# A decoder block on one core: the self attention runs in cycles of two pairs of heads, grouped by kind of work

## What is computed

```python
q = _split_heads(x @ Wq + bq, h)
k = _split_heads(x @ Wk + bk, h)
v = _split_heads(x @ Wv + bv, h)
scale = 1.0 / jnp.sqrt(jnp.float32(ATTN_DIM))
pattern = jnp.einsum('bhid,bhjd->bhij', k, q) * scale
prob = jax.nn.softmax(pattern, axis=-2)
out = jnp.einsum('bhis,bhid->bhsd', prob, v)
b, _, s, dv = out.shape
concat = out.transpose(0, 2, 1, 3).reshape(b, s, h * dv)
return concat @ Wo + bo
...
x = x + _L0_attn_ref(_layernorm(x, axis=-1), ...)
x = x + _L0_xattn_ref(_layernorm(x, axis=-1), ctx_1024, ctx_1024, mask_1x1xSxS2_ik1, ...)
x = x + _L0_ffn_ref(_layernorm(x, axis=-1), ...)
```

## Time and profile before

| | us |
|---|---|
| median of 3 runs | 214.42 |
| lowest and highest | 214.04, 215.87 |
| the profiled execution | 215.71 |
| its span, first to last instruction | 213.9 |
| TensorE busy in it | 198.1 (93%) |
| VectorE busy | 161.6 (76%) |
| ScalarE busy | 127.9 (60%) |
| GpSimd busy | 93.1 (44%) |

### The profile page before, as it was taken

The page is one execution under the profiler, slowest core; times in us unless marked ns, Lnnn a source line. Parts: engine busy times, 40 slices in busy tenths (PEclk is TensorE's granted clock), DMA queues, the critical chain, the costliest instruction groups (busy, mean ns, idle before and its releaser), DMA issues.

```text
span 213.9 us, 4341 instructions
## 1 busy us (share of the span) xinstructions
PE 198.1 (93%) x1544; PEld 149.2 (70%) x1544; DVE 161.6 (76%) x424; ACT 127.9 (60%) x300; POOL 93.1 (44%) x138
## 2 busy tenths in 40 slices
PE   7799997999999898997969999999898999999993
PEld 6388775676776575655637566566576899999993
DVE  2477558968685996788997999998994676458752
ACT  2385348757575556547947999999696532362320
POOL 7699935664646646205999600000120004611422
PEclk9999999999999999999996999999999999999999
DMA  6950478969945215006004100000000000000000
GB/s 204 359 162 0 150 98 93 96 70 112 122 60 166 78 40 112 0 0 222 3 14 101 34 0 3 0 5 2 0 3 0 3 0 2 3 0 28 0 0 25
DMA packets 10732, 12.67 MB, mean 59 GB/s; under 512 B 864, under 2 KB 8544, under 8 KB 10640
## 3 DMA queue, kind: packets, MB, share of 16 engines
q1 hardware_dynamic: 9896, 11.15, 26.0%
q10 hardware_dynamic: 720, 1.06, 1.5%
q0 software_dynamic: 96, 0.20, 0.4%
HBM read 10.96 MB, written 1.44 MB: 58 GB/s over the span
## 4 chain that ended last, share of the span: by engine, by line
PE 77%; DVE 12%; issue 4%; DMA 2%; POOL 1%; ACT 1%; SPq 0%; POOLq 0%; DVEq 0%
PE ps L844 12%; PE ps L806 10%; PE ps L735 7%; PE ps L865 7%; PE ps L722 7%; PE ps L750 6%; PE ps L784 6%; PE ps L766 6%; PE ps L639 5%; PE ps L652 4%; DVE q_t L1062 3%; DMA wk<-in_L_xattn_Wk 2%; PE ps L621 2%; DVE prob_t L1135 1%; DVE low L1052 1%
## 5 line engine op out<-in xcount | busy, mean ns | idle before, releaser
L444 POOL TENSOR_TENSOR prob<-prob,rec 128x512 f32<-128x512 f32 x32 | 32.6, 1039 | 24.2 <-DVE rec L1117 24.2
L1062 DVE CUSTOM_DVE_ANT_0 q_t<-ps,mask_add 128x512 f32<-128x512 f32 x64 | 41.3, 681 | 1.7 <-PE ps L766 1.7
L544 ACT ACTIVATE prob<-ps,low 128x256 f32<-128x256 f32 x64 | 29.5, 474 | 18.4 <-DVE low L1052 18.4
L569 ACT ACTIVATE q_t<-q_t,low 128x512 f32<-128x512 f32 x44 | 29.4, 719 | 9.8 <-DVE low L1062 9.8
L381 POOL TENSOR_SCALAR var_eps<-mean_var 128x2 f32<-128x2 f32 (+1 forms) x5 | 1.1, 224 | 64.3 <-DVE mean_var L921 64.3
L806 PE MATMUL ps<-ident,q_t 128*128 128x128 f32 x176 | 23.3, 274 | 3.8 <-DVE place_o L1135 1.9
L806 PEld LDWEIGHTS ps<-ident,q_t 128*128 128x128 f32 x176 | 20.0, 141 | 8.7 <-issue 4.5
L1052 DVE TENSOR_REDUCE low<-ps 128x2 f32<-128x512 f32 x32 | 20.5, 683 | 6.3 <-PE ps L722 6.3
L554 ACT ACTIVATE q_t<-ps 128x512 f32<-128x512 f32 x18 | 10.6, 598 | 21.0 <-PE ps L844 21.0
L1132 DVE COPY prob_t<-ps 128x512 f32<-128x512 f32 x32 | 20.5, 680 | 1.5 <-PE ps L750 1.5
L766 PE MATMUL ps<-k_stack,q_stack 72*128 72x512 bf16 x64 | 19.6, 391 | 1.3 <-issue 1.3
(11 more groups left out here) (165 smaller groups left out, 424.8 us busy)
## 6 DMA issues: line engine op xcount, KB each, us to landing
k_stack<-k_dram SPq DMA_DIRECT2D x9, 256.0 KB
q_stack<-q_dram SPq DMA_DIRECT2D x6, 192.0 KB
wg<-in_L_ffn_w_gate SPq DMA_DIRECT2D x1, 1024.0 KB, 28.8
wu<-in_L_ffn_w_up SPq DMA_DIRECT2D x1, 1024.0 KB, 35.7
k_dram<-prob SPq DMA_DIRECT2D x1, 768.0 KB, 5.2
...
```

What stands on the lines that cost most here:

```text
L444: nc.gpsimd.tensor_tensor(pr, pr, rec1[:, s % 2, r, :].unsqueeze(2).to_broadcast([P, C, S]), ALU.mult).then_inc(s_norm1, 1)
L544: e = nc.scalar.activation(prob1[:, s % 3, r, c * S:(c + 1) * S], ps[:, 2 * (s % 2) + r, c * S:(c + 1) * S], ACT.Exp, bias=low1[:, s % 2, ...
L569: nc.scalar.activation(prob2[n % 3][:, c, :], score2[n % 2][:, c, :], ACT.Exp, bias=low2[:, n % 2, c:c + 1], scale=-1.0).then_inc(s_exp2, 1)
L1062: nc.vector.tensor_tensor_reduce(out=score2[n % 2][:, c, :], in0=ps[:, 2 * (n % 2) + c, :], in1=mask_add[:, c, :], scale=1.0, scalar=3e38, ...
```

## The change

Self attention now advances in cycles of two pairs, on every even g up to 16. In a cycle TensorE does the scores of pairs g and g+1, the transposes of pair g-2, the output projections of two pairs, the transposes of pair g-1, and then the value products of pairs g-2 and g-1. The values of an odd pair go into `PT_BANK` (bank 4) rather than bank 6, so the next transposes into that bank wait for ScalarE to have read them. Of the four copies of transposed probabilities in a cycle, ScalarE makes the one of pair g-2, r = 1; VectorE makes three. VectorE's order is: four row minima, the copy of pair g-2, r = 0, the reciprocals of pair g, both copies of pair g-1, what `BETWEEN` adds, the reciprocals of pair g+1. GpSimd divides both pairs of a cycle before it takes up what `BETWEEN` adds. The number of matmuls, exponentials, reductions and DMAs stays the same.

```diff
--- before.py
+++ after.py
@@ -111,9 +111,18 @@
 
 
 
-WO1 = {p + LAG_V + 1: [(0, p)] for p in range(NP)}
+WO1 = {}
 for p in range(NP):
-    WO1.setdefault(max(NP + p + LAG_V + 1, 14 + p // 2), []).append((1, p))
+    WO1.setdefault(p - p % 2 + 4, []).append((0, p))
+for p in range(NP):
+    WO1.setdefault(max(NP + p - p % 2 + 4, 14 + p // 2), []).append((1, p))
+
+O1_BANK = (O_BANK, PT_BANK)
+
+
+def cycle(g):
+
+    return g % 2 == 0 and g <= N_SELF
 
 
 def items():
@@ -294,7 +303,7 @@
         s_kparts, s_qparts, s_maskadd = map(sem, ("s_kparts", "s_qparts", "s_maskadd"))
         s_xbo, s_x1, s_x1bo, s_x2 = map(sem, ("s_xbo", "s_x1", "s_x1bo", "s_x2"))
         s_score1, s_low1, s_exp1, s_rec1, s_norm1 = map(sem, ("s_score1", "s_low1", "s_exp1", "s_rec1", "s_norm1"))
-        s_turn1, s_pt1, s_pv1, s_o1 = map(sem, ("s_turn1", "s_pt1", "s_pv1", "s_o1"))
+        s_turn1, s_pt1, s_pt1a, s_pv1, s_o1 = map(sem, ("s_turn1", "s_pt1", "s_pt1a", "s_pv1", "s_o1"))
         s_wo, s_q2ps = map(sem, ("s_wo", "s_q2ps"))
         s_v2 = sem("s_v2")
         s_score2, s_low2, s_exp2 = map(sem, ("s_score2", "s_low2", "s_exp2"))
@@ -446,8 +455,9 @@
 
             for g in range(LAST_G + 2):
                 n = g - N_SELF
-                if 1 <= g <= N_SELF:
-                    divide1(g - 1)
+                if cycle(g) and g < N_SELF:
+                    divide1(g)
+                    divide1(g + 1)
                 for kind, b, _ in BETWEEN.get(g, ()):
                     if kind == "residual":
                         reciprocal_std(1 + b, b * C, C)
@@ -547,6 +557,16 @@
                                                  accum_out=sum1[:, s % 2, r, c:c + 1])
                     e.then_inc(s_exp1, 1)
 
+            def probs_evac(s, r):
+                act.wait_ge(s_turn1, 2 * s + r + 1)
+                nc.scalar.copy(prob1_t[:, s % 2, r, :], ps[:, PT_BANK + r, :]).then_inc(s_pt1a, 1)
+
+            def outputs1(s):
+                b, p = divmod(s, NP)
+                act.wait_ge(s_pv1, s + 1)
+                nc.scalar.activation(o1_t[:, b, p, :], ps[:, O1_BANK[s % 2], 0:S], ACT.Identity,
+                                     bias=bias1[:, 2, p:p + 1]).then_inc(s_o1, 1)
+
             def silu_step(i):
                 act.wait_ge(s_g, i + 1)
                 if i >= 2:
@@ -573,12 +593,23 @@
                 n = g - N_SELF
                 if g == 0:
                     values_evac(g)
-                for what in BETWEEN.get(g, ()):
-                    between(what)
-                if g < N_SELF:
-                    exp1(g)
-                if g == 1:
-                    values_evac(g)
+                if cycle(g):
+                    if g < N_SELF:
+                        exp1(g)
+                    if g == 0:
+                        values_evac(1)
+                    if g >= 2:
+                        probs_evac(g - 2, 1)
+                    for what in BETWEEN.get(g, ()):
+                        between(what)
+                    if g < N_SELF:
+                        exp1(g + 1)
+                    if g >= 2:
+                        outputs1(g - 2)
+                        outputs1(g - 1)
+                else:
+                    for what in BETWEEN.get(g, ()):
+                        between(what)
                 if n in O_READY:
                     k = O_READY[n]
                     act.wait_ge(s_pv2, k + 1)
@@ -587,11 +618,6 @@
                     nc.scalar.copy(o_raw[:, :], ps[:, O2_BANK[k], 0:S]).then_inc(s_oraw, 1)
                 if 0 <= n < N_CROSS:
                     exp2(n)
-                if 0 <= g - LAG_V < N_SELF:
-                    b, p = divmod(g - LAG_V, NP)
-                    act.wait_ge(s_pv1, g - LAG_V + 1)
-                    nc.scalar.activation(o1_t[:, b, p, :], ps[:, O_BANK, 0:S], ACT.Identity,
-                                         bias=bias1[:, 2, p:p + 1]).then_inc(s_o1, 1)
                 if 0 <= n - LAG_T < N_CROSS:
                     act.wait_ge(s_turn2b, n - LAG_T + 1)
                     nc.scalar.copy(prob2_t[(n - LAG_T) % PT_SLOTS][:, 2:4, :],
@@ -724,15 +750,27 @@
                                   k1_t[rows, p, b * S:(b + 1) * S], start=True, stop=True)
                     last.then_inc(s_score1, 1)
 
+            def copied_by_dve(s, r):
+
+                pe.wait_ge(s_pt1, 3 * (s // 2) + 1 + (r + 1) * (s % 2))
+
+            def copied(s, r):
+
+                if r == 1 and s % 2 == 0:
+                    pe.wait_ge(s_pt1a, s // 2 + 1)
+                else:
+                    copied_by_dve(s, r)
+
             def values1(s):
                 b, p = divmod(s, NP)
-                pe.wait_ge(s_pt1, 2 * (s + 1))
-                if s >= 1:
-                    pe.wait_ge(s_o1, s)
+                copied_by_dve(s, 0)
+                copied(s, 1)
+                if s >= 2 and s % 2 == 0:
+                    pe.wait_ge(s_o1, s - 1)
                 for c in range(C):
                     for r in range(2):
                         h = 2 * p + r
-                        last = mm(ps[HD1 * r:HD1 * (r + 1), O_BANK, 0:S],
+                        last = mm(ps[HD1 * r:HD1 * (r + 1), O1_BANK[s % 2], 0:S],
                                   v1[:, b * C + c, h * HD1:(h + 1) * HD1],
                                   prob1_t[:, s % 2, r, c * S:(c + 1) * S], start=c == 0, stop=c == C - 1)
                 last.then_inc(s_pv1, 1)
@@ -741,7 +779,9 @@
                 for r in range(2):
                     pe.wait_ge(s_norm1, 2 * s + r + 1)
                     if s >= 1:
-                        pe.wait_ge(s_pt1, 2 * (s - 1) + r + 1)
+                        copied(s - 1, r)
+                        if s % 2 == 0 and r == 0:
+                            pe.wait_ge(s_o1, s)
                     elif r == 0:
                         pe.wait_ge(s_vev[0], NC_)
                         pe.wait_ge(s_vev[1], NC_)
@@ -799,7 +839,8 @@
                     if n >= 1:
                         pe.wait_ge(free, n)
                     else:
-                        pe.wait_ge(s_pt1, 2 * N_SELF)
+                        copied(N_SELF - 1, half)
+                        pe.wait_ge(s_o1, N_SELF)
                     for k2 in range(2):
                         kc = 2 * half + k2
                         for c in range(C):
@@ -874,22 +915,26 @@
                 if g == 0:
 
                     values_of_tokens(0)
-                if g < N_SELF:
+                if cycle(g) and g < N_SELF:
                     scores1(g)
+                    scores1(g + 1)
                 if 1 <= n + 1 < N_CROSS:
                     scores2(n + 1)
-                if g >= 1 and g in V_ITEMS:
-                    values_of_tokens(g)
+                if g == 0:
+                    values_of_tokens(1)
+                if cycle(g) and g >= 2:
+                    turn1(g - 2)
                 for b, p in WO1.get(g, ()):
                     out_proj1(b, p)
                 for what in BETWEEN.get(g, ()):
                     between(what)
-                if 0 <= g - LAG_T < N_SELF:
-                    turn1(g - LAG_T)
+                if cycle(g) and g >= 2:
+                    turn1(g - 1)
                 if 0 <= n - LAG_T < N_CROSS:
                     turn2(n - LAG_T)
-                if 0 <= g - LAG_V < N_SELF:
-                    values1(g - LAG_V)
+                if cycle(g) and g >= 2:
+                    values1(g - 2)
+                    values1(g - 1)
                 if n + 1 == 0:
                     scores2(0)
                 if FFN_G <= g < FFN_G + FFN_EARLY:
@@ -1107,29 +1152,41 @@
                 for what in FFN_BETWEEN.get(i, ()):
                     between(what)
 
+            def reciprocals1(s):
+                for r in range(2):
+                    dve.wait_ge(s_exp1, 2 * s + r + 1)
+                    if s >= 2:
+                        dve.wait_ge(s_norm1, 2 * (s - 2) + r + 1)
+                    nc.vector.reciprocal(rec1[:, s % 2, r, :], sum1[:, s % 2, r, :]).then_inc(s_rec1, 1)
+
+            def probs_evac(s, r):
+                dve.wait_ge(s_turn1, 2 * s + r + 1)
+                nc.vector.tensor_copy(prob1_t[:, s % 2, r, :], ps[:, PT_BANK + r, :]).then_inc(s_pt1, 1)
+
             dve.wait_ge(s_maskadd, 1)
             dve.wait_ge(s_const, 1 + NE)
             for g in range(LAST_G + 1):
                 n = g - N_SELF
-                if 1 <= g <= N_SELF:
-                    for r in range(2):
-                        dve.wait_ge(s_exp1, 2 * (g - 1) + r + 1)
-                        nc.vector.reciprocal(rec1[:, (g - 1) % 2, r, :], sum1[:, (g - 1) % 2, r, :]
-                                             ).then_inc(s_rec1, 1)
                 if g == 0:
                     values_evac(g)
-                if g < N_SELF:
+                if cycle(g) and g < N_SELF:
                     low_scores1(g)
-                if g == 1:
-                    values_evac(g)
+                    low_scores1(g + 1)
+                if g == 0:
```

(14 more changed lines are left out.)

## The result

The changed kernel took 221.0 us (median of four runs, 219.15 to 223.81) and the kernel before, run with it, 214.77 (also four). The ratio is 1.0246, with a 95% interval of 1.0188 to 1.0305: slower by some 6 us, where 4.5 had been forecast; whether by more than 2% the interval leaves open. Every ratio in this document leaves out the slow executions, those more than 1.5% above the fastest of the same kernel (here the one of 223.81 us, with the early query seven of twelve), while every median takes in all of them. The profiled execution took 219.15 us, its span is 217.3.

What follows compares the result with a forecast made beforehand. TensorE was taken as the bound (77% of the chain). Fill +1.6, four cycles +1.1, with layer norm and query +5.4 in all, less 0.9 given back: +4.5 us on the median 214.42, forecast 218.9, range 215.0 to 221.0.

Steps and rivals of the forecast that it cites:

- A: Main case, a chain of latencies in self attention, fill, layer norm and query: 218.9 us, own range 216.6 to 220.9, chance 0.58.
- The wait in the cycle: Transposes of pair g-2 wait 0.5 us for VectorE's copy behind four row minima; two-pair cycle about 7.5 us, not 6.85.
- TensorE's saving: Self attention: fewer changes of kind cut TensorE's own two-pair work from 7.20 us to 6.85, perhaps about 6.6.
- ScalarE's copy: ScalarE's one copy per cycle takes about 0.6 us, and even 0.94 would be covered before its transposes are due.
- Fill: Start of self attention: the scores of pair 4 come 1.6 us later, at 40.6.
- Layer norm and query: Pair 12's cycle: x_hat waits behind both GpSimd divisions, row minima start at 2.95, cycle grows 1.8 us, delaying the query.
- The DRAM trip: The query's round trip from q_t to the first cross scores takes 10.70 us, as before.
- Given back: From first cross scores to the residual of batch 1: less work left, 10.2 us instead of 11.1, so -0.9.
- rival B: The main chain plus one more clock drop, costing 1.2 us: 220.1 us, chance 0.16.
- C: Rival: copy in time, cycles of 6.85, but start, layer norm and DRAM trip losses stay: 215.0 us, chance 0.15.
- D: Rival: TensorE stays the bound everywhere, copy starting before about 3.1, eight cycles save 2.8 to 4.8: 210.6 us, chance 0.11.

Runs made afterwards that it cites:

- early query: Quiet GpSimd kernel with batch 0's query product behind the transposes of pair 11 and its split ahead of pair 13's reciprocals: 214.48 us, ratio 0.9858.
- four kinds: Kernel before, with the projection of eight steps moved behind the value products, so TensorE changes kind four times a pair: 220.07 us, ratio 1.0129.
- new start: Changed kernel with pair 0's reciprocals ahead of VectorE's V copies and pair 1's exponentials ahead of ScalarE's: 221.6 us, ratio 1.0174.
- `rstd` first: Changed kernel with GpSimd working out batch 0's rstd between the divisions of pairs 10 and 11: 221.81 us, ratio 1.0332.
- quiet GpSimd: Three mends kernel, with GpSimd also waiting for batch 0's x_hat before dividing pair 11: 215.26 us, ratio 0.9891.
- fillers: Changed kernel plus unused identity matmuls, 11 in the cycle of pair 12 and six ahead of the first cross scores: 219.52 us, ratio 1.0169.
- the last: Early query kernel plus unused identity matmuls, four in the cycle of pair 12 and eight ahead of the cross scores: 212.21 us, ratio 0.9815.
- three mends: Changed kernel with first copy ahead of the fourth row minimum, rstd between two divisions, and the other order at the start: 217.99 us, ratio 1.0128.
- late weights: Changed kernel with four of SyncE's five expert weight loads moved behind batch 0's query DMAs: 221.41 us, ratio 1.0206.

## Why the prediction was right, and where it was short

**The number was right at the very edge.** The range ended at 221.0 and the median is 221.0; the four runs of the same kernel behind it have 221.05. That it fell inside is luck. The four runs lie 6.2 us above the kernel before, where 4.5 had been forecast. (The upper end of A's own range was also added too low: its terms, 0.8, 0.5 and 1, give 221.2 and not 220.9.) What follows says which terms held.

**The wait in the cycle: right.** The copy was forecast to start at 3.58, the transposes at 4.41, the next copy at 5.08, the cycle to take 7.53. Measured 3.57, 4.39, 5.06 and 7.51. That it is the cause, and not more work on TensorE, is shown by moving the copy alone (7.51 to 6.97).

**TensorE's saving: right in size.** I had 6.85 for its work alone. With the copy in time the cycle is 6.97, in which the value products still wait a little for their copy. In the experiment with four kinds, one change more made a step 0.15 us longer (3.60 to 3.75). An estimate from that: three changes fewer (transposes and projections, both 128*128 in the profile, are one kind) are 0.45, and 7.20 - 0.45 = 6.75, if each is worth the same, which no run shows. The pieces of the 6.97 in the trace with the copy moved come close to it: from start to start 2.04, 0.92, 0.90, 1.15 and 1.96, and with second transposes as short as the first it would be 6.74. What makes a change of kind cost anything the traces don't show. The saving was real (7.20 to 6.97), and smaller than the 0.54 that the late copy took.

**ScalarE's copy: right.** It took 0.60, was covered, and without it the cycle stays the same.

**Fill: right** (+1.50 for +1.6). Half is the order of V's copies (0.78 in the experiment).

**Layer norm and query: right in place and nearly in size.** VectorE came to the row minima at +2.90 (forecast 2.95), `q_t` at +9.97 (10.05). The DRAM trip took 10.99 (10.70), and TensorE was through with its work at about +19.4 (19.3).

**Given back: right.** From the first cross scores to the residual 10.1 instead of 11.1, forecast -0.9. So the residual was 4.6 late, forecast 4.5. Up to here the two profiles hold no drop of the clock, and all terms of the sum are borne out.

**The term that was too small is the one on the clock.** The sum was made against a profiled execution of before that holds one drop, on the assumption that after has one too; one drop more was rival B, at 0.16 and 1.2 us. The 1.2 was an estimate from the 3.4 us at 0.50 in the earlier trace rows; the runs showed 1.1 to 1.7 for one. The changed kernel's profiled execution had none, and behind the residual it took 1.2 less than before. In its other executions there were more. A drop lasts 3.4 us, so a mean clock of 0.992 over some 217 us is one (3.4 x 0.5 / 217 = 0.008), 0.984 two, 0.977 three. The eight executions of the changed kernel have 1.0, 0.984, 0.984, 0.985, 0.969, 0.977, 0.992 and 1.0, about 1.75 drops on average; of the 53 executions of before that were run beside the experiments, 46 have 0.991 or 0.992, and one of 231.22 us has 0.852. The times follow: with 0.992 or more the changed kernel took 218.53 to 219.15 us, with less 220.43 to 223.81.

What a drop costs depends on its place: 1.13 us in the cycle with `x_hat`, 1.2 behind the residual; one recorded near 8 us did not make pair 0 later than in the other execution of the same kernel. From first cross scores to the residual of batch 1 the profiles of two-pair cycles fall into three kinds: 10.10 with none (the changed kernel, and those with the new start, `rstd` first, quiet GpSimd, fillers, and the last), 11.75 with a drop of 3.4 us (copy moved, three mends, early query, the changed kernel again), 13.0 to 13.2 with 6.8 us (all copies on VectorE, late weights). So a drop there is 1.65, a double one 3.0. With the one drop of before, at 1.2, the changed kernel's 219.15 becomes 220.35, close to the 220.2 of the sum. A drop behind the wait for the cross scores instead makes it 220.8, both together 222.0, and the three of the execution repeated above 223.1; it took 223.09. The likeliest case should have been A with B in it. I had reckoned with over 2 us of idle time for TensorE in the cycle with `x_hat` (the profile has one wait of 2.64), but set it aside as shorter than the sparse stretch of 3.90 us in the earlier trace rows. Half clock follows in one execution on 1.26 us busy of 3.40, and in six profiles behind waits of 1.7 to 2.6 us for the cross scores, while in two others waits of 1.94 and 2.00 us passed without it. Why it follows in some executions and not in others the runs don't show.

What stays open is the rest of the spread. With fillers and a clock of 0.992 or better, runs still went up to 223.58. The gap inside the value products is a part of it, seen in three profiled executions: with the fillers pair 12 comes at 74.00 instead of 70.61, for the gap and the drop behind it. That it is a late packet of instructions is argued from the times at which both come and from the place in the program, not shown: the one experiment on it moved only part of the traffic.

**C and D** fell with the first cycle. D's condition was a copy at 3.1 or earlier: with the copy at 2.97 the cycle is 0.23 shorter than two pairs of before, 1.8 us over eight, where D counted 2.8. With the other losses mended the ratios are 0.9858 and 0.9815. But an earlier query, fillers and `rstd` in another place were not tried on the kernel before, so how much of this the grouping itself brings is not shown.
